# A two-layer graph kernel on one core: adjacencies kept as bytes, one output product moved ahead, and half of another made in the tail

## What is computed

```python
# layer one
D = abs(x[:, :, None, :] - x[:, None, :, :])
h = einsum('bijc,oc->bijo', D, W1) + b1             # 64 outputs for each pair of nodes
h = leaky(batchnorm(h)); s = einsum('bijo,uo->biju', h, W2)[..., 0] + b2[0]
A = softmax(where(adj > 0, s, NEG), axis=-1)
y = leaky(batchnorm((A @ x) @ Wg.T + bg))
out = concatenate([x, y], axis=2) @ Wt.T + bt
# layer two
h = x @ W; dense = leaky(h @ a1 + swapaxes(h @ a2, 1, 2))
out = elu(softmax(where(adj > 0, dense, NEG), axis=1) @ h)
```

## Time and profile before

| what | us |
|---|---|
| median of three runs (lowest, highest) | 1186.64 (1182.36, 1191.24) |
| the profiled execution's own time | 1189.32 |
| its span, first to last instruction | 1187.5 |
| pass one, to its last product | 665 |
| changeover, to ACT's first activation of pass two | 675.6 |
| pass two, to the last scores | 1012.1 |
| tail, to the end of the batch norm of y | 1067.1 |
| layer two | 120.4 |

### The profile page before, as it was taken

The page is one execution under the profiler, slowest core; times in us unless marked ns, Lnnn a source line. Parts: engine busy times, 40 slices in busy tenths (PEclk is TensorE's granted clock), DMA queues, the critical chain, the costliest instruction groups (busy, mean ns, idle before and its releaser), DMA issues.

```text
span 1187.5 us, 17527 instructions
## 1 busy us (share of the span) xinstructions
PE 1062.9 (90%) x6376; PEld 463.2 (39%) x6376; DVE 1058.1 (89%) x1418; ACT 994.8 (84%) x1238; POOL 541.3 (46%) x251
## 2 busy tenths in 40 slices
PE   3889999999999999999999599999999999548997
PEld 1333333333333333333333212333333333338886
DVE  6899999999999999999999787999999999435787
ACT  3879999999999899999999599898988989006987
POOL 6466667666666666666667101111122211261331
PEclk9989999999999999999999799999999999758998
DMA  6324343434343334343434789999999998700222
GB/s 165 131 118 177 143 173 146 178 142 164 156 178 142 160 160 177 142 168 152 178 142 188 299 305 358 366 355 360 349 358 350 347 348 296 191 4 12 71 80 72
DMA packets 118005, 237.52 MB, mean 200 GB/s; under 512 B 17568, under 2 KB 65952, under 8 KB 117920
## 3 DMA queue, kind: packets, MB, share of 16 engines
q1 hardware_dynamic: 116336, 235.70, 54.6%
q10 hardware_dynamic: 1584, 0.69, 0.3%
HBM read 126.52 MB, written 109.84 MB: 199 GB/s over the span
## 4 chain that ended last, share of the span: by engine, by line
PE 45%; DVE 32%; ACT 9%; issue 7%; DMA 3%; POOL 2%; SPq 1%; POOLq 0%; DVEq 0%; ACTq 0%
PE psum L708 18%; DVE store L275 12%; PE psum L718 11%; PE psum L722 8%; DVE plain_st L979 4%; ACT store L610 3%; ACT store L556 3%; DVE store L1058 3%; DMA early<-score_rows 2%; PE psum L821 1%; PE psum L680 1%; PE psum L698 1%; PE psum L778 1%; PE psum L855 1%; POOL store L475 1%
## 5 line engine op out<-in xcount | busy, mean ns | idle before, releaser
L708 PE MATMUL psum<-store,w1tt_sb 128*64 128x512 f32 x1792 | 426.0, 605 | 37.4 <-ACT store L556 19.2
L275 POOL TENSOR_TENSOR store<-h_ext 128x2048 f32<-128x2048 f32 (+1 forms) x96 | 386.5, 4028 | 140.9 <-PE psum L708 137.0
L275 DVE TENSOR_TENSOR store<-psum,h_ext 128x2048 f32<-128x2048 f32 x160 | 364.0, 2275 | 0.9 <-ACT h_ext L526 0.9
L556 ACT ACTIVATE store<-store 128x2048 f32<-128x2048 f32 x160 | 305.1, 1929 | 15.2 <-DVE store L275 10.3
L708 PEld LDWEIGHTS psum<-store,w1tt_sb 128*64 128x64 f32 x1792 | 121.7, 137 | 277.5 <-issue 223.5
L610 ACT ACTIVATE store<-store,st 128x1024 f32<-128x1024 f32 x192 | 225.8, 1242 | 1.4 <-DVE st L1045 1.4
L718 PE MATMUL psum<-store,w_twice 128*64 128x512 f32 x768 | 201.5, 603 | 3.9 <-DVE early L944 3.5
L979 DVE BATCH_NORM_STATS2 plain_st<-store 128x6 f32<-128x512 f32 x256 | 160.6, 678 | 0.6 <-ACT store L568 0.6
L722 PE MATMUL psum<-early 128*64 128x512 bf16 x1152 | 158.0, 381 | 0.0
L275 DVE TENSOR_TENSOR store<-h_ext 128x2048 f32<-128x2048 f32 x64 | 139.1, 2173 | 2.6 <-PE psum L708 2.6
L778 PE MATMUL psum<-store,w_rows 128*32 128x512 f32 x1024 | 131.8, 606 | 5.4 <-ACT store L610 5.4
(11 more groups left out here) (153 smaller groups left out, 1143.4 us busy)
## 6 DMA issues: line engine op xcount, KB each, us to landing
kept_products<-store SPq DMA_DIRECT2D x192, 512.0 KB, 2.7
store<-kept_products SPq DMA_DIRECT2D x192, 512.0 KB, 7.5
early<-score_skew SPq DMA_DIRECT2D x16, 384.0 KB, 6.4
early<-adj SPq DMA_DIRECT2D x16, 256.0 KB, 8.0
early<-adj_t SPq DMA_DIRECT2D x16, 256.0 KB, 3.0
store<-x SPq DMA_DIRECT2D x16, 256.0 KB, 4.8
out<-early SPq DMA_DIRECT2D x16, 256.0 KB, 2.4
score_rows<-early SPq DMA_DIRECT2D x64, 32.0 KB, 3.7
```

The source lines that it names most:

```text
L275: return engine.tensor_tensor(t[:, :, 0:steps, :], nodes.unsqueeze(2).broadcast_to([C, 2, steps, N]), windows(h_ext[:, 2 * c, :], STEP * m ...
L556: nc.scalar.activation(t, t, ACT.Abs).then_inc(abs_ready, 1)
L708: last = nc.tensor.matmul(t[MID * g:MID * g + MID, b, :], w1tt_sb[:, 0:MID], diff[slot][:, g, b * BANK:b * BANK + BANK], start=True, stop= ...
```

## The change

*Adjacencies.* They are loaded in pass one (both layouts in turn, one quad behind each couple's store of chunk 5), and GpSimd turns them into bytes that stay in SBUF (`edges`, at chunk 2 of a couple). `mask` and the loads of pass two and layer two are gone; `mask_l1` multiplies bytes and has eight slots. The split parts of the node products live in a ring of four couples to make room.

*Score rows.* They are transposed where they lie (four 128x128 transposes) and put in order by four strided DVE instructions; the store and load between are gone.

*Weighted nodes.* The nodes are multiplied by Wg ahead of the mixing (`weighted_nodes` on PE, `nodes_out` on ACT, six quads in the changeover and ten at the odd positions 1 to 19 of pass two), so that `att_mix` gives y: `att_out` and the copy of mix are gone, and `att_y` reads bank 4.

*Changeover.* The first PLAIN chunk is made again at the end of pass one; ACT sums all but the last couple's statistics ahead, and does not wait for `pass2_ready`.

*Tail and layer two.* For eight quads the h part of the outputs is made in the tail and added to x (`outputs_of_x`, `fold_x`). x is loaded from the last chunks on. In layer two `outputs` stands ahead of `values` and `attend`, and the exponential of elu reads PSUM at once.

```diff
-        EVAC, DIST_T, TURN, SUM, SCORES, EXP, NORM, TURN_P, COPY, MIX, MIX_COPY, OUT, Y = \
-            19, 32, 33, 50, 52, 56, 58, 61, 62, 64, 65, 67, 69
-        STORE_ROWS, LOAD_DIST, STORE_SKEW, LOAD_HALF, LOAD_ADJ = 21, 26, 35, 41, 30
-        TAIL = 72
+        EVAC, DIST_T, TURN, SUM, SCORES, EXP, NORM, TURN_P, COPY, MIX, Y = 19, 21, 22, 37, 39, 43, 45, 48, 49, 51, 52
+        STORE_SKEW, LOAD_HALF = 24, 30
+        TAIL = 55
+        EARLY_MIX = 6
+        PRE, PRE_AT = 8, CHUNKS + 7
...
@@ SP, pass one
+            def load_adj(v):
+
+                if v >= 2:
+                    sp.wait_ge(edges_set, v - 1)
+                sp.dma_start(adj_sb[v % 2], (adj_n, adj_tn)[v % 2][:, quad(v // 2), :]).then_inc(adj_in, 16)
+
+            load_adj(0)
             for k in range(NKEPT):
                 sp.wait_ge(kept_ready, k + 1)
                 sp.dma_start(kept_dram[k, :, :], kept[k % ZRING]).then_inc(kept_stored[k % ZRING], 16)
+                c, r = divmod(k, len(KEPT))
+                if KEPT[r] == 5 and c + 1 < COUPLES:
+                    load_adj(c + 1)
...
@@ SP, pass two
+                if n == CHUNKS + AHEAD - 1:
+                    for q in range(PRE):
+                        load_x(q)
...
@@ GpSimd
+            def edges(v):
+                pool.wait_ge(adj_in, 16 * (v + 1))
+                nc.gpsimd.tensor_scalar(no_edge[v % 2][:, quad(v // 2), :], adj_sb[v % 2], 0.0, None, ALU.is_le)\
+                  .then_inc(edges_set, 1)
...
                 if n % PER in POOLED:
                     differences(n)
+                if n % PER == 2:
+                    edges(n // PER)
...
@@ ACT, changeover
+            sums(0, most, (20, 21, 25))
+            nodes_out(0)
+            nodes_out(1)
             act.wait_ge(counted, NPLAIN)
             act.wait_ge(copies_counted, NCOPIED)
+            sums(most, NCOUNTED, (22, 23, 26)).then_inc(stat_squares, 1)
+            for u in range(2, EARLY_MIX):
+                nodes_out(u)
 
             act.wait_ge(stat_bias, 1)
...
-            act.wait_ge(pass2_ready, 1)
             for n in range(CHUNKS + TAIL):
                 if n < CHUNKS:
                     activate(n)
+                if mix_at(n) is not None:
+                    nodes_out(mix_at(n))
...
@@ PE
+            def outputs_of_x(j):
+                if j == 0:
+                    pe.wait_ge(leaky_ready, CHUNKS)
+                elif j >= 4:
+                    pe.wait_ge(x_folded, j - 3)
+                for b in range(QUAD):
+                    last = nc.tensor.matmul(bank(j % 4)[:, b, :], h_ext[:, QUAD * j + b, 0:N], wt1_sb[:, :],
+                                            start=True, stop=True)
+                last.then_inc(x_out, 1)
...
             def at_zero(n):
 
-                for s, step in ((s_masked, SCORES), (mix_ready, MIX_COPY)):
+                pe.wait_ge(weighted_ready, NQ)
+                for s, step in ((s_masked, SCORES), (y_ready, Y)):
                     if so_far(step, n) > 0:
                         pe.wait_ge(s, so_far(step, n))
...
-                for lag, do in ((TURN2, turn2), (DENSE, dense), (MASKED, values), (ATTEND, attend), (-1, outputs)):
+                for lag, do in ((TURN2, turn2), (DENSE, dense), (-1, outputs), (MASKED, values), (ATTEND, attend)):
...
@@ DVE
+            def fold_x(j):
+                dve.wait_ge(x_out, j + 1)
+                dve.wait_ge(x_bt, j + 1)
+                nc.vector.tensor_tensor(X[j], bank(j % 4), X[j], ALU.add).then_inc(x_folded, 1)
+
             for n in range(-LEAD_DIFF, CHUNKS + TAIL):
+                if 0 <= n - PRE_AT - 1 < PRE:
+                    fold_x(n - PRE_AT - 1)
```

More of the change, by code:

```diff
@@ L146, in two_layers @@
         s_rows = late(0, 512)
[L147 to L155, removed]
+        s_turn = by_graph(late(512, 256))
+        s_half = by_graph(late(768, 768))
+        s_shift = by_graph(late(1536, 512))
+        prob = by_graph(late(2048, 512))
+        prob_tr = by_graph(late(2560, 512))
+        adj_sb = [by_graph(late(3584 + 512 * t, 512).bitcast(I32)) for t in range(2)]
         ln_st = sb("ln_st", [128, B, 6])
@@ L587, in _, with nodes_out, sums @@
                     take(m)
+            def nodes_out(u):
+                if u == 0:
+                    act.wait_ge(placed, NQ - 1)
+                act.wait_ge(weighted, u + 1)
+                nc.scalar.copy(h_nat[:, quad(u), :], nodes_bank(u)).then_inc(weighted_ready, 1)
+            def sums(first, last, to):
+                n = 4 * (last - first)
+                part = lambda k: counted_part(k)[:, 4 * first:4 * last]
+                dumps = ((28, 0), (30, 0), (28, 0)) if first == 0 else ((28, 800), (30, 800), (28, 900))
+                for k, (of, how, more) in enumerate(((2, ACT.Identity, {}), (1, ACT.Square, dict(scale=16.0, bias=sc(5))),
+                                                     (1, ACT.Identity, dict(scale=256.0)))):
+                    tile, at = dumps[k]
+                    if k == 2 and first == 0:
+                        act.wait_ge(deviations, 1)
+                    done = nc.scalar.activation(tiles(tile, 2)[:, at:at + n], part(of), how, accum_out=sc(to[k]), **more)
+                    if k == 0 and first == 0:
+                        done.then_inc(deviations, 1)
+                return done
+            most = NCOUNTED - len(COUNTED)
+            act.wait_ge(counted, NPLAIN - len(PLAIN))
+            act.wait_ge(copies_counted, NCOPIED - len(COPIED))
+            sums(0, most, (20, 21, 25))
+            nodes_out(0)
+            nodes_out(1)
             act.wait_ge(counted, NPLAIN)
             act.wait_ge(copies_counted, NCOPIED)
[L591 to L593 removed]
+            sums(most, NCOUNTED, (22, 23, 26)).then_inc(stat_squares, 1)
+            for u in range(2, EARLY_MIX):
+                nodes_out(u)
             act.wait_ge(stat_bias, 1)
@@ L788, in at_one @@
             def at_one(n):
-                for s, step in ((turn_ready, TURN), (prob_tr_ready, COPY), (y_ready, Y)):
+                pe.wait_ge(weighted_ready, NQ)
+                for s, step in ((turn_ready, TURN), (prob_tr_ready, COPY)):
                     if so_far(step, n) > 0:
@@ L843, in _ @@
                     scores(m // 2)
-                for step, do in ((DIST_T, turn_dist), (SUM, att_sum), (TURN_P, att_turn), (MIX, att_mix), (OUT, att_out)):
+                if 0 <= n - PRE_AT < PRE:
+                    outputs_of_x(n - PRE_AT)
+                for step, do in ((DIST_T, turn_dist), (SUM, att_sum), (TURN_P, att_turn), (MIX, att_mix)):
                     j = quad_at(n, step)
```

277 lines of the change are left out of this document (133 added, 144 removed).

## The result

The kernel after takes 1182.58 us (median of 20 runs, 1180.48 to 1184.03) against 1188.13 of before beside it (20 runs): ratio 0.995, interval 0.9939 to 0.996. That is 0.5% faster, inside the 1% that the prediction calls no change, 4.6 us above its 1178.0. The profiled execution took 1181.9 us, span 1180.1.

What follows compares the result with a forecast made beforehand. No single engine was taken to bound the whole; pass two was bound by DVE in program order. +5 + 17 - 19 - 12 = -9 gave 1180.3 us profiled, median 1178; range 1150 to 1198.

Steps and rivals of the forecast that it cites:

- The whole: All stages of the kernel: terms summing to -9 us, 1180.3 us for the profiled execution, median 1178.
- Pass one, +5: Pass one: added adjacency loads and GpSimd conversions make it 5 us longer, bounds 0 to +25.
- The sign for the worse: Pass one: GpSimd's load waits of over 5 us a couple, with late differences, would show the forecast too fast.
- Rival 2: Pass one: GpSimd decides, late loads delay conversions and differences; 1216 us at 5.0 us landings, 1200 at 4.5; chance 0.14.
- Changeover and start of pass two, +2.3: From pass one's end to the third row copy: 2.3 us longer, with ten more weighted groups on PE.
- Per quad, +1.06: Pass two: each quad 1.06 us longer, 22.5 us, as DVE stands 2.16 us for PE's sum; twelve quads +12.7.
- Rival 1: Pass two: the sum of the halves does not hold up DVE; a quad takes 20.4 us, whole 1150; chance 0.15.
- Tail, -19: After the last scores: 36 us in place of 55, bounds 32 to 43.
- The ports' price: Tail: 1.8 us because SCORES' subtraction runs against GpSimd's x_and_bias.
- The clock's: Tail: 1.5 us for PE at its lower level in part.
- Layer two, -12: Layer two: outputs moved ahead open the loop, steps of 5.6 then 6.1 us; 12 us shorter, bounds -6 to -16.
- Rival 3: Layer two and tail give half, -6 and -14, as DVE takes the loop's place; whole 1189 us; chance 0.17.

Runs made afterwards that it cites:

- w1_no_groups: Kernel after without the ten weighted groups of nodes in pass two, so quads 6 to 15 are mixed with unweighted nodes: 1173.72 us.
- p1_loads_earlier: Kernel after with the adjacency loads issued one couple earlier, with a semaphore for each of the two buffers: 1168.98 us, ratio 0.983.
- b1_scales_on_pool: Kernel before with the layer norm's small scale product made by GpSimd instead of VectorE, nothing else changed: 1183.09 us, ratio 0.9946.

## Why the prediction was right, point by point

- **The whole**: -9 forecast, -7.4 in the profiled spans. The four stages came out with the forecast's signs, but that the sum is so close is luck: errors of +10 in pass two, -5 in layer two, -1.7 in pass one and -1.4 in the tail nearly cancel, and pass one hides two terms of 12 and 9 us. (The 1029 for the last scores leaves out the forecast's own +5; by its terms it is 1034, and it came at 1042.4.)
- **Pass one, +5 for +3.3: right number by luck.** The step was a cycle over a quad of two landings at 4.0 us and two conversions at 1.95, which gives 0.72 us a quad, sixteen times; at 1.5 us nothing would be left of it. The conversions took 1.49, a load landed after 3.6, and in quads without a normalisation indeed nothing is left (39.28 us). The loads cost 12.1 us all the same. The step that failed is the one cycle for all sixteen quads, with GpSimd's difference and ACT as the only way to the cost: 11.3 of the 12.1 us lie in the stretches with a normalisation, which the working leaves out, where DVE has no time to spare and its small instructions stand in GpSimd's displaced subtractions. ACT's waits for GpSimd's subtraction are there as well (15.4 us between 103 and 640 us, 3.6 before). The sign for the worse, load waits of over 5 us a couple, was there too (5.3). That a gain of 8.8 us, nearly all of it in the first 80 us, would hide the cost was not foreseen. Rival 2 was late loads at a higher price (landings of 4.5 us and more), which did not come.
- **Changeover and start of pass two, +2.3 for +8.5: the mis-sized term.** The working had PE at 7.8 us of work in 9.0 per couple and 11.8 with four groups, which is an excess of 2.8, and then took +1.5 and +1 for the stretch. Leaving the groups out gave 10.0 us, and moving only ACT's copies nothing: there was no slack on PE for them. The first row copy comes 40.6 us behind pass one's last product, 2.3 more than before, and the other 6.2 of the 8.5 us lie between the first and the third. Against them stands the gain that was forecast: ACT's wait of 5.18 us at chunk 2 is gone, and with the groups left out the first row copy comes 34.2 us behind pass one's last product, where before it came 38.3 behind. From the first row copy to the third w1_no_groups takes 40.9 us, before took 38.1. Those 2.8 us fit the attention of quad 0: its scores, normalisation and copy (4.3 us of DVE, positions 39 to 49) now stand ahead of the third row copy (51) and stood behind it. That is read from the positions; no run took it apart. (So the 5.7 us which one expectation names for this was too much, and its effect stays in w1_no_groups.)
- **Per quad, +1.06 for +1.37.** The wait of SCORES on SUM is there in all twelve quads, 2.21 us from Y to SCORES for 2.16. The other 0.3 is in part the mask instruction that meets GpSimd (mean 1317 ns, before 1261, four or five a quad: 0.2 to 0.3). The remaining differences of hundredths were not traced. (Where the working sets 16j+49 against 16j+66, the mix copy of the same quad is at 16j+65; nothing hangs on it.) Rival 1 was wrong as a state of this kernel. As a remedy it gives 0.97 a quad by itself and 1.8 with the other two, 21.0 us; its 20.4 was never reached.
- **Tail, -19 for -20.4.** 34.6 us for 36. The ports' price was forecast at 1.8: SCORES' subtraction took 1.08 and 1.24 us where 0.69 is usual, 0.9 together. The clock's was forecast at 1.5: the mean grant from 1042 to 1077 is 0.81, for 0.66 before. Neither was tested alone.
- **Layer two, -12 for -17.3.** By its own parts: to the first normalisation -3.0 (for -3.1), eight steps -4.9 (for -2.5), the next seven -7.0 (for -3.7), the end -2.6 (for -2.7). The steps went from 6.6 to 5.25 and 5.80 us, where 5.6 and 6.1 were forecast: the term that was mis-sized is PE's own work in a step, 5.80 us for 6.1. Rival 3 did not come: DVE, busy 47.8 of 53 us, did not take the loop's place. The order alone gives 7.6 us and the fold 3.2; if they add, the other 6.5 are the loads and masks of layer two that went and the elu's half, not parted here.

## What to carry to other kernels

A stage that ends where it was forecast can hold two large terms of opposite sign: move one suspected cost by itself before believing the sum. An addition that hides in the mean slack of an engine is charged in full where that engine is already without a gap; read the engine's timeline at that place, not its share. And where GpSimd and VectorE both work from SBUF, what stands beside what decides: here a 0.15 us instruction cost 4 us, a load that landed late cost 12 us, by the traces mostly through another engine's small instructions, and shifting one load by two positions took 0.4 us off each quad. A cycle worked out for the usual quad says nothing of the unusual one: look for the stretch in which the busiest engine has no time left.

## What the runs showed of the hardware

- A tiny two-input DVE instruction on SBUF stood until GpSimd's running two-input instruction was through (4.13 and 3.74 us for 0.15; rows above). The Trainium skill (SBUF — State Buffer, Who interferes with whom) says that a VectorE instruction with two SBUF inputs contends with a GpSimd instruction that reads SBUF, and that the port pair which they share is an exclusive lock; here the trace agrees. Beside the one-input byte conversion, which reads SBUF as well (22.89 to 24.39), the same product took 0.57 and ended at 23.51, before it; in p1_loads_earlier it took 0.16 at 67.38, inside a conversion (66.91 to 68.41). There the traces do not show the block, within what a rough GpSimd span can tell.
- A one-input DVE instruction can stand in the same way: 3.90 us for 0.20 beside GpSimd's subtraction (L956 in b1_scales_on_pool).
- It goes the other way round too: GpSimd's 0.72 us addition took 2.77 when DVE's subtraction had begun 0.10 us before it.
